# Sums of squares from two rounded parts, fewer value-norm matmuls, and the last early query tile split one unit sooner

## The reference

```
xq = rms_norm(x @ wq.T, q_norm_w)    # 2048 features, mean of squares over all of them
xk = rms_norm(x @ wk.T, k_norm_w)    # 512 features
xv = x @ wv.T                        # 512 features
```

## Time and profile before

| | us |
|---|---|
| median of 3 runs (lowest, highest) | 1191.52 (1191.12, 1192.47) |
| profiled execution, own time | 1192.52 |
| its span in the trace | 1190.7 |
| TensorE busy | 1156.7 (97%) |
| VectorE busy | 890.4 (75%) |
| ScalarE busy | 743.8 (62%) |

### The profile page before, as it was taken

One profiled execution on the slowest core, in us unless ns is written; L12 is line 12 of the kernel. 1 busy time (PEld: TensorE's weight loads), 2 busy tenths in 40 slices (PEclk: granted clock), 3 DMA queues, 4 the chain that ended last, 5 costly groups with the idle time before them and its releaser, 6 DMA issues.

```text
span 1190.7 us, 26659 instructions
## 1 busy us (share of the span) xinstructions
PE 1156.7 (97%) x9016; PEld 988.1 (83%) x9016; DVE 890.4 (75%) x2329; ACT 743.8 (62%) x1583; POOL 304.8 (26%) x354
## 2 busy tenths in 40 slices
PE   6999999999899999999999999999999999999997
PEld 5878888887777889898988998898988888888876
DVE  5587878687899888888888888888866575645464
ACT  4655556455899888888888888888853443222230
POOL 3000000000588843324242323233211100202022
PEclk9999999999999999999999999999999999999999
DMA  5316355346667775556655674557435540303020
GB/s 177 106 45 230 160 194 218 119 193 239 201 240 240 250 223 184 170 186 208 205 177 183 205 216 150 165 167 225 139 118 202 168 140 2 107 1 107 1 71 37
DMA packets 100898, 189.55 MB, mean 159 GB/s; under 512 B 9376, under 2 KB 39072, under 8 KB 100768
## 3 DMA queue, kind: packets, MB, share of 16 engines
q1 hardware_dynamic: 100768, 187.88, 47.1%
HBM read 116.22 MB, written 71.63 MB: 158 GB/s over the span
## 4 chain that ended last, share of the span: by engine, by line
PE 90%; DVE 4%; issue 2%; ACT 2%; DMA 0%; POOL 0%; SPq 0%; DVEq 0%; POOLq 0%; ACTq 0%
PE bank L1419 22%; PE bank L1553 19%; PE bank L1484 14%; PE bank L1357 12%; PE bank L1445 11%; PE bank L1463 3%; PE bank L1461 3%; PE bank L1462 3%; PE bank L1473 2%; DVE stats L1021 1%; DVE pT_lo L1181 1%; DVE pT_lo L1177 1%; ACT p_sb L806 1%; DVE u_sb L1058 1%; PE bank L1530 1%
## 5 line engine op out<-in xcount | busy, mean ns | idle before, releaser
L806 ACT ACTIVATE p_sb<-u_sb,low 128x384 f32<-128x384 f32 (+2 forms) x512 | 271.8, 535 | 61.9 <-DVE low L1058 57.7
L1058 DVE CUSTOM_DVE_ANT_0 u_sb<-bank,bias 128x384 f32<-128x384 f32 (+2 forms) x512 | 229.4, 452 | 46.8 <-PE bank L1357 24.4
L1357 PE MATMUL bank<-k_st,q_st 128*128 128x384 f32 (+2 forms) x1024 | 251.7, 328 | 3.1 <-DVE low L1058 3.1
L1445 PE MATMUL bank<-ident,p_sb 128*128 128x128 f32 x1152 | 217.4, 279 | 14.5 <-DVE pT_lo L1177 5.2
L1177 DVE TENSOR_TENSOR pT_lo<-bank,pT_hi 128x384 f16<-128x384 f32 (+2 forms) x394 | 179.0, 454 | 26.9 <-ACT pT_hi L917 18.6
L1357 PEld LDWEIGHTS bank<-k_st,q_st 128*128 128x128 f32 x1024 | 168.6, 191 | 20.0 <-DVE low L1058 3.7
L1445 PEld LDWEIGHTS bank<-ident,p_sb 128*128 128x128 f32 x1152 | 140.7, 141 | 45.7 <-ACT p_sb L806 18.2
L917 ACT ACTIVATE pT_hi<-bank 128x384 f16<-128x384 f32 (+2 forms) x394 | 159.7, 405 | 28.7 <-PE bank L1445 25.1
L699 POOL TENSOR_TENSOR o_out<-o_raw,inv_sum 128x256 f32<-128x256 f32 x128 | 79.9, 626 | 320.8 <-DVE inv_sum L1189 320.8
L1553 PE MATMUL bank<-zT_hi,gu 128*128 128x512 f32 x352 | 139.2, 395 | 0.6 <-DVE hid L1308 0.6
L1553 PE MATMUL bank<-zT_lo,gu 128*128 128x512 f32 x352 | 138.1, 392 | 0.0
(11 more groups left out here) (135 smaller groups left out, 2302.2 us busy)
## 6 DMA issues: line engine op xcount, KB each, us to landing
q_st<-q_scr SPq DMA_DIRECT2D x32, 1024.0 KB, 8.1
q_scr<-qk SPq DMA_DIRECT2D x61, 512.0 KB, 2.7
k_st<-k_scr SPq DMA_DIRECT2D x64, 256.0 KB, 3.3
o_scr<-o_out SPq DMA_DIRECT2D x128, 128.0 KB, 3.8
o_in<-o_scr SPq DMA_DIRECT2D x16, 768.0 KB, 5.2
z_in<-z_scr SPq DMA_DIRECT2D x8, 1024.0 KB, 6.2
k_scr<-qk SPq DMA_DIRECT2D x12, 512.0 KB, 2.7
v_scr<-v_out SPq DMA_DIRECT2D x4, 1040.0 KB, 6.4
```

Of the source, the lines that this page charges most:

```text
L806: nc.scalar.activation(p_sb[:, u % RING, 0:w], u_sb[:, u % RING, 0:w], ACT.Exp, scale=-1.0, bias=low[:, u % RING:u % RING + 1]).then_inc(p ...
L1058: nc.vector.tensor_tensor_reduce(out=u_sb[:, u % RING, 0:w], in0=bank[u % 2][:, 0:w], in1=bias[2 * u // UNITS][:, u % REP, at:at + w], sca ...
L1357: mm = nc.tensor.matmul(bank[u % 2][:, 0:w], q_st[:, s, r, P * i:P * i + P], k_st[:, s, part, P * key:P * key + w], start=(part == 0), sto ...
L1445: mm = nc.tensor.transpose(bank[probability_bank(A)][:, P * j:P * j + P], p_sb[:, u % RING, P * j:P * j + P], ident[:])
```

## The change

It has four parts.

1. **Sums of squares.** ScalarE rounds `sum_sq` to `sum_hi` (`round_sum`), VectorE subtracts it to get `sum_lo` (`split_sum`), and TensorE multiplies both parts by a rounded matrix of ones, `ones_r`, into the same bank. The sums stand one gemm later: after gemms 18 and 21 (before, 17 and 20, and in batch 0 17 and 21). Root and inverse stand one gemm later too.
2. **Value norm.** The four squares are made two gemms earlier, VectorE adds them up (`sum_v`, three additions), and one float32 matmul sums over the partitions.
3. **Last early tile.** ScalarE rounds it at unit 2 and VectorE splits it at unit 4; both were at unit 5.
4. **Buffers.** `sum_lo` lies over the first `square` buffer, so the squares of gemms 1 and 18 wait for the sum before them to be made.

```diff
-ROOT_AT, LATE_INVERSE_AT = (QC + 2, QC + KVC + 1), 4
+SQUARE_V_AT = QC - 3
+SUMS_AT = (QC + 2, QC + KVC + 1)
+ROOT_AT, LATE_INVERSE_AT = (QC + 3, QC + KVC + 2), 4
...
-LAST_EARLY_AT = 5
+LAST_EARLY_AT = (2, 4)
...
+            def round_sum(b, n):
+
+                act.wait_ge(acc_ready, NSQ * b + (NSQ if n else QC - 1))
+                at_least(act, ssq_psum, 2 * b + n)
+                nc.scalar.activation(sum_hi[:], sum_sq[:, n], ACT.Copy).then_inc(sum_hi_ready, 1)
...
-                        if first and n == QC - 1:
+                        if first and n == SQUARE_V_AT:
                             square_v()
...
+                            if n in (1, SUMS_AT[0]):
+                                at_least(act, ssq_psum, 2 * b + n // QC)
...
+                        if n == QC:
+                            round_sum(b, 0)
...
+                        if n == QC + KVC:
+                            round_sum(b, 1)
...
+            def sum_v():
+
+                for k, (to, other) in enumerate(((2, 3), (0, 1), (2, 0))):
+                    dve.wait_ge(v_squared, KC)
+                    if k == 2:
+                        dve.wait_ge(v_summed, 2)
+                    to, other = raw[QC + to], raw[QC + other]
+                    nc.vector.tensor_tensor(to, to, other, ALU.add).then_inc(v_summed, 1)
...
+            def split_sum(b, n):
+                dve.wait_ge(sum_hi_ready, 2 * b + n + 1)
+                nc.vector.tensor_tensor(sum_lo[:], sum_sq[:, n], sum_hi[:].bitcast(F32), ALU.subtract).then_inc(sum_ready, 1)
...
+                        if n == QC + 1:
+                            split_sum(b, 0)
+                        if first and n == SQUARE_V_AT + 1:
+                            sum_v()
                         if first and n == QC + 1:
                             scale_v()
...
+                        if n == QC + KVC + 1:
+                            split_sum(b, 1)
...
-                pe.wait_ge(acc_ready, NSQ * b + (NSQ if n else QC - 1))
-                pe.wait_ge(sq_ready, (QC + KVC) * b + (QC + KVC if n else QC))
+                if n == 0 and isinstance(b, int) and b == 0:
+                    pe.wait_ge(ones_r_ready, 1)
+                pe.wait_ge(sum_ready, 2 * b + n + 1)
...
-                nc.tensor.matmul(bank[6 + n][:], ones[:], sum_sq[:, n], start=True, stop=True).then_inc(ssq_psum, 1)
+                nc.tensor.matmul(bank[6 + n][:], ones_r[:], sum_hi[:], start=True, stop=False)
+                nc.tensor.matmul(bank[6 + n][:], ones_r[:], sum_lo[:], start=False, stop=True).then_inc(ssq_psum, 1)
...
-                        for kc in range(KC):
-                            pe.wait_ge(v_squared, kc + 1)
-                            mm = nc.tensor.matmul(bank[7][:], ones[:], raw[QC + kc], start=(kc == 0), stop=(kc == KC - 1))
-                        mm.then_inc(v_norm_psum, 1)
+                        pe.wait_ge(v_summed, KC - 1)
+                        nc.tensor.matmul(bank[7][:], ones[:], raw[QC + 2], start=True, stop=True).then_inc(v_norm_psum, 1)
...
-                    if n == QC + 1:
-                        sum_squares(b, 0)
-                    if n == QC + KVC + first:
-                        sum_squares(b, 1)
+                    if n in SUMS_AT:
+                        sum_squares(b, SUMS_AT.index(n))
```

More of the change, by code:

```diff
@@ L260, in sandwich_layer @@
             raw_first = sb(s1, "raw_first", [P, LATE_OWN, T])
-            square = sb(s1, "square", [P, 2, T])
+            with ExitStack() as before_sums:
+                square = sb(before_sums, "square", [P, 2, T])
+            sum_lo = sb(s1, "sum_lo", [P, T], F32R)
+            sb(s1, "second_square", [P, T])
             sum_sq = sb(s1, "sum_sq", [P, 2, T])
@@ L270, in sandwich_layer @@
             raw_last = sb(s1, "raw_last", [P, QC + KVC - LATE_OWN, T])
+            sb(s1, "bias_room", [P, REP * WIN + 16])
+            sum_hi = sb(s1, "sum_hi", [P, T], F32R)
+            ones_r = sb(s1, "ones_r", [P, P], F32R)
             raw = [raw_first[:, f] if f < LATE_OWN else raw_last[:, f - LATE_OWN] for f in range(QC + KVC)]
@@ L350, in sandwich_layer @@
         held = sem("held")
+        ones_r_ready, sum_hi_ready, sum_ready = sems("ones_r_ready sum_hi_ready sum_ready")
+        v_summed = sem("v_summed")
         ident_ready = sem("ident_ready")
@@ L667, in _ @@
                                         op=ALU.pow).then_inc(tile_rstd[i], 1)
+            nc.gpsimd.tensor_copy(ones_r[:], ones[:]).then_inc(ones_r_ready, 1)
             pool.wait_ge(gemm_done, 1)
@@ L952, in _ @@
                     unit_work(n, u)
-                    if n == 0 and u == LAST_EARLY_AT:
+                    if n == 0 and u == LAST_EARLY_AT[0]:
                         round_raw(B - 1, LATE - 1)
@@ L1233, in _ @@
                         split_v(B - 1, NGEMM - 1)
-                    if n == 0 and u == LAST_EARLY_AT:
+                    if n == 0 and u == LAST_EARLY_AT[1]:
                         split_raw(B - 1, LATE - 1)
```

## The result

| | before | after |
|---|---|---|
| median of 5 runs (lowest, highest), us | 1191.52 (1189.82, 1192.47) | 1198.90 (1197.93, 1199.18) |
| ratio of the times, with its 95% interval | | 1.0061 (1.0047 to 1.0076) |
| profiled execution, us | 1192.52 | 1198.93 |
| granted TensorE clock, mean over the span | 0.998 | 0.993 |

A forecast was written before the change was run, and what follows sets the result against it. TensorE, busy 97% of the span, was taken as the bound. +4.7 at batch 3's T, -0.6 at the start of attention and +1.7 for the clock gave +5.8, forecast 1197.3 us after the median correction, range 1191 to 1200.

The forecast's parts named there:

- The bound and its margin: Projection stage: TensorE is the bound with nothing ahead of it; block 5's chain has at most 0.35 us of slack.
- What is removed: TensorE: each of eight sums falls from 0.86 to 0.45 us, the value norm from 3.43 to 0.86; together -5.9.
- First wait, +0.8 at gemm 16: Batch 0: TensorE waits about 3.4 us for VectorE's sum_v additions before the value-norm matmul; gemm 16 starts 0.8 later.
- Second wait, 5.75: Batch 0: sum_lo subtraction and later split lengthen block 5's chain; TensorE idles 5.75 us before gemm 20, +6.1 there.
- the one on the clock: Batch 0: one half-clock stretch, +1.7 us, charged behind the 5.75 wait; none behind the 3.4 wait, left open at 0 to 1.7.
- The second sums: Each batch: TensorE waits some 0.35 us before the second sum, nearly its 0.41 saving; batches 1 and 2 give back 0.47 each.
- Start of attention, -0.6: Start of attention: early tile split and later inverse together give -0.5 to -0.6 us, first bias add at T + 10.3.
- The collision with unit 8's scaling: Start of attention: VectorE's scaling of unit 8 waits beside GpSimd's bias product, paying about 1.2 us.
- The worse one: Rival, chance 0.12: half clock behind both waits, late second sums lose 0.5 each in batches 1 to 3; +9, 1200.5 us.
- the forecast's own variant: Half-clock loss behind both batch 0 waits: +7.5, 1199.0 us; given 0.25 of the forecast's 0.64.
- No waits: Rival, chance 0.08: both batch 0 waits do not appear, TensorE's -5.9 reaches the end, early tile split adds -1.6; 1184 us.
- no change: Rival, chance 0.16: one term much smaller, such as a second wait of 2 us without clock loss; +0.4, 1192 us.

The follow-up runs named there:

- the best version: Kernel before with early tile split, two-part sums, old value norm, new places for sum_lo subtractions, last batch's second sum in float32: 1187.57 us.
- the two runs that part the places: Changed kernel with only the first sum_lo subtraction behind the value-weight scaling: 1192.80 us; with only block 5's split ahead of gemm 18's addition: 1198.23 us.
- the version with both places of block 5's chain moved back: Changed kernel with the first sum_lo subtraction behind the value-weight scaling and block 5's split ahead of gemm 18's addition: 1191.95 us.
- the value-norm run: Kernel before with the value-norm part alone: earlier squares, three additions, one matmul; 1195.41 us.
- best-with-norm version: The best version plus value norm by one matmul, its additions ahead of block 4's split, input statistics two gemms later: 1189.57 us.
- the best version with the late root: The best version with the last batch's second sum in two parts behind gemm 21, root and inverse behind it: 1188.93 us.
- the last run: Changed kernel with the last early tile rounded and split at unit 5 again, as before: 1202.61 us.

## Why the prediction was right, and where its sizes were off

- **The bound and its margin.** Right. Block 5's chain had 0.35 of slack, and everything that the change took from TensorE in batch 0 was lost on that chain.
- **What is removed.** Right: a sum in two parts takes 0.46 (two starts 0.23 apart, 72.53 to 72.99), and the second sums' share arrived where nothing waited (0.83 per batch in the best version).
- **First wait, +0.8 at gemm 16.** The wait was 3.2 for 3.4 on the prediction's count (61.55 - 58.37; the profile's bracket says 3.02), and the three additions took the time forecast. But the one matmul of the value norm takes 2.01 of the chain, not 0.86, since it ran at the low clock. Of the 1.15 between them some 0.24 had been counted in the wait (0.3 from the end of the last addition to the matmul, where 0.06 shows: 59.41 + 2.08 = 61.49, and 61.55). The other 0.9 I put down to the clock. Counted from TensorE's arrival, gemm 16 started 1.75 late (63.55 - 62.65 + 0.85).
- **Second wait, 5.75.** It was 5.3, from the mechanism forecast: the order on VectorE (shown by the two runs that part the places), with the reciprocal at 69.37 for 68.7 (70.2 with the 0.85 that this execution was ahead). Of the chain's steps none was off by more than 0.3, except that gemm 16 itself ran 0.64 longer by the clock (its copy starts at 67.12, 3.57 behind gemm 16's start, for 2.93). Gemm 20 started at +7.4 on the same count, not +6.1.
- **The step that failed is the one on the clock**: "Behind the wait of 3.4 it is open, 0 to 1.7; I take 0", and one stretch of 1.7 behind the other. The rows show a loss behind both: 0.9 on the value norm's matmul, 0.8 on gemms 16 to 18 (8.98 - 8.18), 2.4 on gemms 20 and 21 (7.86 - 5.45). The 0.9 and 0.64 of the 0.8 delay block 5's chain. So the clock cost 3.9 where 1.7 stood, 2.2 more; the steps of the chain and the second sum of batch 0 gave 0.3 each back, which leaves the 1.6 between 7.4 and 5.8. The Trainium skill (TensorE: Matmul & The Clock Gate, What's actually happening) has the throttled rate as the default, released by activity; by that both waits were to be charged, and the trace agrees for these two.
- **A row that the prediction does not use.** The 192 matmuls from 13.28 take 46.10 in the trace of before, where 192 x 0.227 are 43.6. TensorE's timeline of before has the missing 2.5 at the start of the kernel, behind the first idle times (6.16, 1.61, 0.35 and 0.86): starts 0.43 apart until 18.11, twice the usual distance, although the granted clock of these windows is given as 1.00. So that trace had slow matmuls behind idle time in two places, not one.

```profile
14.70 0.63 PE L1419 MATMUL bank<-xT_hi,w_hi 128*128 128x512 f32 x1
15.13 0.63 PE L1419 MATMUL bank<-xT_hi,w_lo 128*128 128x512 f32 x1
```

- **The second sums.** Right within 0.1: 0.38 of wait for about 0.35, and a batch's period shorter by 0.50 (94.03 to 162.41 is 68.38, before 68.88) for 0.47. Only in batch 0 the second sum cost 0.3 less than taken.
- **Start of attention, -0.6.** Right in sum (-0.7) and partly by luck. The first bias addition at T + 10.3 and the tile split at 0.69 are as forecast. The collision with unit 8's scaling did not occur: the scaling came 7.0 behind the first bias addition (308.50 - 301.50), just as GpSimd was done, for the 5.8 forecast, since the bias additions before it were held up by TensorE at half clock. With the tile split alone the clock was full, the scaling came after 6.15 and the collision did occur, at half the price. What was not seen is that the tile split by itself also removes the half-clock stretch: it does so alone, and not inside the change, where the late inverse leaves a gap of its own (1.44, and 0.57 behind it).
- **The execution that was read.** 1.0 was taken off, because before's profiled execution stood above its median. It came late to batch 0's end: its chain starts the value norm at 59.38, and the four other kernels that leave that place as it was start it at 58.42 to 59.02. With the 0.85 between before and after counted, the traces give 7.4 too, so the subtraction was right in size.
- **Rivals.** The worse one had the loss behind both waits and +9; the forecast's own variant, loss behind both and nothing else, said 1199.0, and 1198.9 was measured. "No waits" and "no change" fell with the two waits; the version with both places of block 5's chain moved back shows what "no change" would have needed (1191.95).

**What stays open.** Why the other executions of the value-norm run had a lower mean clock than its profiled one; and why TensorE's waits of 1.6 and 1.9 in the best-with-norm version left the clock at 1.00, while 3.0 did not. At the start of attention it even fell behind shorter ones: behind 1.44 in after, and behind 1.66 in the best version with the late root. The rows show where, not what decides it. No run has the late inverse at the full clock, so what kept the scaling of unit 8 clear of GpSimd is read from the timelines alone. A version without the wait for `raw_last` and with VectorE relieved in batch 0 was not tried.

## What to carry to other kernels

Before something is taken from the engine that is the bound, find the chain with the least slack behind it, and look at what the edit puts ahead of that chain's members on the in-order engines: a subtraction of 0.69 us that has to wait for TensorE's next gemm held up a reciprocal that was ready, and cost 6 us. Charge a new idle time of TensorE like these two (3.0 and 5.3 us, inside dense matmuls) with the half-clock stretch behind it (here 1.7 and 2.4 us on top). And an edit in several parts deserves a run of each: one part here was worth -2.7, and with it and new places for another the kernel became 0.4% faster than before.

## What the runs showed of the hardware

- **A wait of 3.0 us inside dense matmuls is enough for the low clock.** All six kernels that have this wait (3.0 to 3.2) show it: their granted clock over 62 to 64 was 0.50 to 0.64. Before the change a gap of 2.83 at the start of attention had shown it, and the half pace at the start of the kernel. Gaps of 1.6 and 1.9 in batch 0 left it at 1.00. But the length of the gap does not decide alone: a gap of 2.83 in the value-norm run left it at 1.00 in the profiled execution (window 302 to 306 above), and gaps of 1.44 (after) and 1.66 (best, last root late) at the start of attention, with small matmuls and smaller gaps behind them, were followed by 0.57 and 0.50. The Trainium skill (TensorE: Matmul & The Clock Gate, What's actually happening) says that the number of slow matmuls at a kernel's start varies from run to run of one kernel; here it varies in the middle too (gemms 16 to 18 took 8.98 in after and 10.00 in the last run).
- **VectorE beside GpSimd.** Three slow instructions with two SBUF inputs end 0.55 after the bias product does: 299.96 against 299.41, 299.94 against 299.39 in the run with the tile split alone, 309.60 against 309.05 in the last run; in four more runs it is 0.54 to 0.56. That is a VectorE instruction that does most of its work only when GpSimd has finished. The Trainium skill (SBUF — State Buffer, Who interferes with whom) has it blocked for GpSimd's whole length, and the three agree to within 0.2. So the price is what is left of GpSimd's instruction, and a short overlap costs little: 0.63 here for an overlap of 0.83.
- **The start scatters.** The same instructions of batch 0 lie up to 1.0 us apart from one execution to the next. Differences below 1 us at a place are to be read as distances from an earlier mark of the same trace.
